# Zero padding of two short contraction parts (64 and 48 rows) to 128 rows in a two-layer decoder kernel

## The reference

```python
# layer 1 attention (latent): T = 128 tokens, 16 heads, HEAD_DIM = 128 + 64
q = rmsnorm(hidden @ q_a_w, q_a_ln_w) @ q_b_w        # 256 -> 192 -> 16 * 192
kv_raw = hidden @ kv_a_w                             # 64 latent + 16 * 64 rope
kv_latent = rmsnorm(kv_raw[..., :64], kv_a_ln_w)
kv = (kv_latent @ kv_b_w).reshape(B, T, 16, 128 + 128)
scores = einsum('bqhd,bkhd->bhqk', q, concat(k_nope, k_rope)) * scale
...
return attn @ o_w

# layer 1 feed forward (mixture), I = 176, 8 experts, top 2
shared_out = sigmoid(x @ shared_gate.T) * (x @ shared_up.T) @ shared_down.T   # contraction over 176
return x + shared_out + routed
x = _layernorm(x + ...)
```

## Time and profile before

| | |
|---|---|
| median of 3 runs | 1812.41 us |
| the three runs | 1812.41, 1830.32, 1805.54 us |
| profiled execution | 1830.32 us, span 1830.1 us |
| PE busy | 1487.3 us (81%), 9568 matmuls |
| DVE, ACT, POOL busy | 944.2, 585.0, 498.8 us |
| mean granted TensorE clock | 0.868 of full speed |

### The profile page before, as it was taken

The page is one execution under the profiler, slowest core; times in us unless marked ns, Lnnn a source line. Parts: engine busy times, 40 slices in busy tenths (PEclk is TensorE's granted clock), DMA queues, the critical chain, the costliest instruction groups (busy, mean ns, idle before and its releaser), DMA issues. The chain is left out here.

```text
span 1830.1 us, 33017 instructions
## 1 busy us (share of the span) xinstructions
PE 1487.3 (81%) x9568; PEld 1027.2 (56%) x9568; DVE 944.2 (52%) x2501; ACT 585.0 (32%) x1370; POOL 498.8 (27%) x1027
## 2 busy tenths in 40 slices
PE   1563899699996444439999999999999699997897
PEld 1562566355553222217788778888787355553565
DVE  6874465355553899952334324232234355553776
ACT  1464344144442222212222212222122144443453
POOL 6343477321211222221212211131112122221232
PEclk7677899799999676667999979797889699998999
DMA  8289565322221001020001000010000222221111
GB/s 239 80 255 232 161 200 176 99 78 77 86 77 41 26 26 32 26 64 4 18 21 32 17 17 22 18 29 17 17 14 27 69 84 78 85 79 59 35 47 42
DMA packets 148702, 128.43 MB, mean 70 GB/s; under 512 B 13360, under 2 KB 127344, under 8 KB 148640
## 3 DMA queue, kind: packets, MB, share of 16 engines
q1 hardware_dynamic: 142880, 116.46, 21.6%
q0 software_dynamic: 4320, 10.88, 2.3%
q10 hardware_dynamic: 1440, 0.33, 0.1%
HBM read 83.59 MB, written 46.20 MB: 71 GB/s over the span
## 5 line engine op out<-in xcount | busy, mean ns | idle before, releaser
L412 DVE TENSOR_REDUCE ca_nm<-ca_p_s 128x2 f32<-128x512 f32 x256 | 176.1, 690 | 223.4 <-PE ca_p_s L320 219.9
L355 PE MATMUL ca_p_o<-ca_pt,ca_va 128*32 128x256 f32 x1024 | 254.1, 386 | 0.7 <-ACT ca_pt L545 0.7
L545 ACT ACTIVATE ca_pt<-ca_p_e 128x512 f32<-128x512 f32 x256 | 152.1, 597 | 162.3 <-PE ca_p_e L342 160.9
L1945 PE MATMUL la_p_f<-la_qt,q_w 128*128 128x128 f32 x512 | 142.8, 366 | 13.2 <-ACT la_lt L2094 11.9
L355 PEld LDWEIGHTS ca_p_o<-ca_pt,ca_va 128*32 128x32 f32 x1024 | 90.9, 109 | 103.8 <-issue 46.3
L1946 PE MATMUL la_p_f<-la_qt,q_w 64*128 64x128 f32 x512 | 144.5, 368 | 0.0
L340 PE MATMUL ca_p_e<-ca_qs,ca_ks 96*128 96x256 bf16 x512 | 128.5, 277 | 0.1
L342 PE MATMUL ca_p_e<-ca_mt,row_of 96*128 96x256 bf16 x512 | 126.8, 274 | 0.0
L320 PE MATMUL ca_p_s<-ca_ks,ca_qs 96*128 96x256 bf16 x512 | 101.8, 283 | 28.2 <-DMA ca_ks<-k_stack 26.3
L2113 ACT ACTIVATE la_pq<-la_p_s,la_nm 128x128 f32<-128x128 f32 x256 | 73.0, 368 | 153.9 <-DVE la_nm L2153 153.9
L1945 PEld LDWEIGHTS la_p_f<-la_qt,q_w 128*128 128x128 f32 x512 | 88.7, 217 | 50.0 <-ACT la_lt L2094 16.9
(11 more groups left out here) (301 smaller groups left out, 3275.9 us busy)
## 6 DMA issues: line engine op xcount, KB each, us to landing
ca_qs<-q_stack SPq DMA_DIRECT2D x64, 192.0 KB, 2.6
ca_ks<-k_stack SPq DMA_DIRECT2D x64, 192.0 KB, 2.9
k_stack<-qkv_stack SPq DMA_DIRECT2D x16, 384.0 KB, 3.1
qa_stack<-qkv_stack SPq DMA_DIRECT2D x16, 384.0 KB, 3.3
ka_stack<-qkv_stack SPq DMA_DIRECT2D x16, 384.0 KB, 3.3
sa_qs<-qa_stack SPq DMA_DIRECT2D x32, 192.0 KB, 2.6
sa_ks<-ka_stack SPq DMA_DIRECT2D x32, 192.0 KB, 3.0
ca_ct<-in_ctx_t SPq DMA_DIRECT2D x32, 128.0 KB, 3.1
```

The source lines that it names most:

```text
L355: last = pe.matmul(p_o[rows, h // 4, :], VA[u][:, kc, h, :], PT[h % 2][:, kc, :], start=(kc == 0), stop=(kc == 1))
L412: dve.tensor_reduce(NM[u][:, h, :], p_s[h % 2][:, :, :], AX.X, ALU.max, negate=True).then_inc(max_done, 1)
L545: act.activation(PT[h % 2][:, :, :], p_e[h % 2][:, :, :], ACT.Exp, scale=SCALE).then_inc(exp_done, 1)
L1945: pe.matmul(bank[:, 128 * j:128 * j + 128], sh.q_w[:, 0, h, :], QT[:, 0, :], start=True, stop=False)
```

## The change

The 64-row part of the query products and the 48-row part of the shared down product get 128 rows, with zeros in the rows that are new. `sh.q_w` gets its upper half of part 1 set to zero once, in preparation, by POOL; `QN` is widened to 256 columns whose last 64 are set to zero once, so that its second transpose gives 128 rows; ACT copies both parts to `QT` with one instruction. In the mixture `SD`'s second part is set to zero ahead of its load, which therefore moves behind a wait on POOL and behind the load of `XR[0]`; `HS` is widened in the same way, and ACT copies `HST` with one instruction. The waits on the constants are raised to match.

```diff
@@ set_constants
+        pool.memset(sh.q_w[64:128, 1, :, :], 0.0).then_inc(const_set, 1)
+        pool.wait_ge(const_set, CONSTANTS)
-CONSTANTS = 16
+CONSTANTS = 17
@@ latent_attention
-        QN = sb("qn", [S, Q_LORA], F32)
+        QN = sb("qn", [S, 2 * 128], F32)
@@ pe: f4
+                if is_first(b):
+                    pe.wait_ge(const_ready, 3)
-                pe.transpose(p_f[0][0:64, 128:256], QN[:, 128:Q_LORA], sh.ident[:, :])
+                pe.transpose(p_f[0][:, 128:256], QN[:, 128:256], sh.ident[:, :])
@@ pe: queries
-                    last = pe.matmul(bank[:, 128 * j:128 * j + 128], sh.q_w[0:64, 1, h, :], QT[0:64, 1, :],
+                    last = pe.matmul(bank[:, 128 * j:128 * j + 128], sh.q_w[:, 1, h, :], QT[:, 1, :],
                                      start=False, stop=True)
@@ act: f4
-                act.activation(QT[:, 0, :], p_f[0][:, 0:128], ACT.Copy)
-                act.activation(QT[0:64, 1, :], p_f[0][0:64, 128:256], ACT.Copy)
+                act.activation(QT[:, :, :], p_f[0][:, 0:256].rearrange("p (c s) -> p c s", c=2), ACT.Copy)
@@ dve: norm_qa
-                dve.tensor_scalar(QN[:, :], ...)
+                dve.tensor_scalar(QN[:, 0:Q_LORA], ...)
@@ pool
+            pool.memset(QN[:, Q_LORA:256], 0.0).then_inc(const_ready, 1)
-            pool.wait_ge(const_ready, 2)
+            pool.wait_ge(const_ready, 3)
@@ mixture_feed_forward
-        HS = sb("hs", [S, EI], F32)
+        HS = sb("hs", [S, 2 * 128], F32)
@@ sp
+            sp.dma_start(XR[0][:, :], x_in[0]).then_inc(xr_loaded[0], 16)
+            sp.wait_ge(const_steps, 4)
             sp.dma_start(SD[0:EI - 128, 1, :], shared_down_t[128:EI]).then_inc(weights_loaded, 16)
-            sp.dma_start(XR[0][:, :], x_in[0]).then_inc(xr_loaded[0], 16)
@@ pe: turn_inner, down
-                    pe.transpose(p_k[0:EI - 128, 128:256], HS[:, 128:EI], sh.ident[:, :])
+                    pe.transpose(p_k[:, 128:256], HS[:, 128:256], sh.ident[:, :])
-                pe.matmul(p_x[:, 1, :], HST[0:EI - 128, 1, :], SD[0:EI - 128, 1, :], start=False,
+                pe.matmul(p_x[:, 1, :], HST[:, 1, :], SD[:, 1, :], start=False,
@@ act: copy_inner
-                    act.activation(HST[:, 0, :], p_k[:, 0:128], ACT.Copy)
-                    act.activation(HST[0:EI - 128, 1, :], p_k[0:EI - 128, 128:256], ACT.Copy).then_inc(inner_copied, 1)
+                    act.activation(HST[:, :, :], p_k[:, 0:256].rearrange("p (c s) -> p c s", c=2),
+                                   ACT.Copy).then_inc(inner_copied, 1)
@@ dve: inner_shared
-                dve.tensor_tensor(HS[:, :], p_s[:, EI:2 * EI], SSIG[:, :], ALU.mult).then_inc(shared_inner, 1)
+                dve.tensor_tensor(HS[:, 0:EI], p_s[:, EI:2 * EI], SSIG[:, :], ALU.mult).then_inc(shared_inner, 1)
@@ dve, pool
-            dve.wait_ge(const_steps, 2)
+            dve.wait_ge(const_steps, 4)
+            pool.memset(SD[:, 1, :], 0.0).then_inc(const_steps, 1)
+            pool.memset(HS[:, EI:256], 0.0).then_inc(const_steps, 1)
-            pool.wait_ge(const_steps, 2)
+            pool.wait_ge(const_steps, 4)
```

More of the change, by code:

```diff
@@ L2160, in norm_qa @@
                 wait(dve, pv_done, G * (b - 1))
-                dve.tensor_scalar(QN[:, :], p_f[1][:, 0:Q_LORA], RQ[:, 0:1], SCALE, ALU.mult, ALU.mult).then_inc(qa_normed, 1)
+                dve.tensor_scalar(QN[:, 0:Q_LORA], p_f[1][:, 0:Q_LORA], RQ[:, 0:1], SCALE, ALU.mult, ALU.mult).then_inc(qa_normed, 1)
                 dve.scalar_tensor_tensor(LL[u][:, 0:2 * LATENT].rearrange("p (n l) -> p n l", n=2),
```

## The result

The changed kernel takes 1685.35 us in the median of three runs (1680.31 to 1685.76), against 1812.41 before: ratio 0.9278, 95% interval 0.9223 to 0.9334. The profiled execution took 1680.31 us, with a span of 1678.5: 151.6 us less than the 1830.1 of before, where 144.7 us were forecast.

A forecast was written before the change was run, and what follows sets the result against it. PE was taken to set the latent stage's pace. Query stage 140.5, copy 1.0 and mixture 5.8, less 2.1 for the memset and 0.5 for the load, made 144.7 us: 1830.3 to 1685.6 us, range 1660 to 1716.

The forecast's parts named there:

- 0.19 us for each change between 64 and 128 rows: Latent query matmuls: each step between 64 and 128 rows costs 0.19 us beyond the pace of equal rows.
- Query matmuls at 0.115 us: Latent query stage: 64 padded matmuls at the rope's pace take 7.36 us, not 13.29; 5.93 us gained a batch.
- The falls of the clock: Latent query stages: no falls at the rope's density; four batches gain 15.28 us each, the first 14.2.
- The price of a fall: Latent batches: one holding a fall of the clock takes 43.92 us in place of 34.58, so 9.35 us.
- the falls stay: Rival, chance 0.08: the drains go but the clock still falls in some query stages; 1714 us.
- The reading that spread and falls are one: Runs before differ by falls in query stages, so the changed median is 1685 us; otherwise near 1668.
- No new wait: Latent batch of about 28.6 us: no new wait priced; as a rival, chance 0.04, about 1701 us.
- The columns: Transpose ahead of the queries: 64 stationary columns cost no more than 128, so widening costs and gains nothing.
- The mixture: Shared down product: 0.30 us and a merged copy's 0.06 gained a batch, 5.8 us; later load at start costs 0.5.
- Preparation: POOL's memset of q_w and a wait behind it put 2.1 us on the path, bounds 0 to 4.
- that nothing changes: Rival, chance 0.03: rows are free in query matmuls, padding saves nothing; 1812 us at the median.
- that full arrays lower the clock: Rival, chance 0.02: 128 active rows in all query matmuls hold the lower clock through the latent stage; 2060 us.

The follow-up runs named there:

- e1: The kernel before with only the changed kernel's part up to the latent stage, the mixture left old: 1685.91 us, ratio 0.934.
- e3: The kernel before, unpadded, reordered so that in each four heads the 128-row products go first, then the 64-row ones: 1706.76 us, ratio 0.946.
- e5: The kernel before with the first query product of each head also on 64 rows, the rest of its contraction left out: 1734.76 us, ratio 0.952.
- e9: The changed kernel with each head's second query product cut to 32 columns and not added to the first: 1759.29 us, ratio 0.966.
- e2: The kernel before with only the mixture's part of the change, the latent stage left old: 1819.72 us, ratio 1.010.
- e7: The changed kernel with each head's 32 weighing columns in both cross attentions put into 128, zero elsewhere: 1643.68 us, ratio 0.907.
- e6b: The changed kernel with POOL's memset of q_w moved behind the issues of the weight loads: 1681.96 us.

## Why the prediction was right

- **The step on which all rests, 0.19 us for each change between 64 and 128 rows, held.** It was read from starts in PE's timeline; `e1` shows that the latent part alone gives all but 4 to 5 us of the gain, and `e3` that the price goes with the changes and not with the 64-row matmul. Query matmuls at 0.115 us: measured 0.112, as a stage without the change is 6.09 us shorter and not 5.93. Eleven batches: 67.0 us against 65.2.
- **The falls of the clock went, as said**: four batches went from 43.92 to 28.21 us, 62.8 us against 61.1, and the first stage gave 14.4 against 14.2. The price of a fall was read a little low: 43.92 was set against 34.58, but the batches that hold the falls are of the kind that takes 34.35, so a fall cost 9.57 us and not 9.35.
- **The slow stretches outside the query stages were not in the sum.** The prediction said that the clock never falls in the stage's rope, score or projection matmuls. In the last batch it does: PE waits up to 0.89 us ahead of its weighings and then runs about ten us at clock 0.50, the projection among them. Another slow stretch lies behind the first query stage (1.5 us gained). These are the windows of the last batch from its last query matmul on, before and after:

```profile
1401.96:1433.10 31.14, 24.28 (x133) 20.54 (x132) 12.29 (x29) 5.64 (x18) 4.67 (x9) 0.82 0.06 18
```

```profile
1257.64:1285.20 27.56, 20.04 (x134) 17.27 (x131) 12.31 (x29) 5.64 (x18) 4.70 (x10) 0.98 0.07 20
```

  Both carry the same work; 3.6 us went with the clock. With some 0.5 us of copies and 0.6 lost at the stage's start the latent stage gained 149.1 us where 141.5 were forecast.
- **The agreement of the medians to 0.3 us is luck.** On the two profiled executions, for which the sum was made, it fell 6.9 us short: 7.6 too little for the latent stage, 1.5 too much for the mixture, 0.5 for preparation, and 1.3 us in stages that the change does not touch. The profiled execution of the changed kernel happened to be its fastest, 5 us below the median.
- **The reason for the clock was half right.** The prediction put it down to PE's density, and rival "the falls stay" to the wait or the weighing. `e5` and `e9` show that the rows in use matter by themselves. The forecast came out because padding mends both at once, and that is luck too. Had the change removed the standstills by using 64 rows throughout, the same reasoning would have missed some 50 us (`e5`: 1734.76 us).
- **The reading that spread and falls are one was borne out**, by `e2` and by the clocks of the runs of before: it is why 1685 was given and not 1668.
- **No new wait came.** PE's wait ahead of the queries fell from 0.82 to 0.78 us; 0.06 was put down, 0.04 measured. The widened transpose cost nothing.
- **The columns.** The prediction said that the trace agrees with the Trainium skill's rule of draining ("TensorEngine Tiling (Array Packing)", Key Properties) for rows and not for columns, by the single case of 64 columns in a transpose. That was too wide. That case stays free, but `e9` shows 12.04 - 7.22 = 4.82 us for 32 changes between 128 and 32 columns, 0.15 us each, and `e7` a gain where they go. For those the trace agrees with the rule.
- **The mixture was sized too high, and its start too low**: 5.8 - 0.5 = 5.3 us forecast, 3.8 measured in its stage. PE's timeline, to be set beside the earlier trace rows:

```profile
1592.29 0.60 PE L2508 MATMUL mf_p_x<-mf_sd,mf_hst 128*128 128x256 f32 x2
1592.72 0.60 PE L2509 MATMUL mf_p_x<-mf_sd,mf_hst 128*128 128x256 f32 x2
1593.15 0.61 PE L2489 MATMUL mf_p_h<-identb,mf_he 128*128 128x128 bf16 x8
...
1596.25 1.47 PE L2465 MATMUL mf_p_s<-mf_ws,mf_xt 128*128 128x360 f32 x4 [0.52 <-ACT mf_xt L2541]
```

  The pair of pairs takes 0.86 us as said, 0.30 less. The batch went from 7.97 to 7.66 us (L2508 to L2508, the next at 1599.95), 0.31 and not 0.36, 5.0 us over sixteen: ACT's merged copy did not add to it. At the start of the stage PE waits for the same load as in the earlier trace rows:

```profile
1545.07 2.74 PE L2465 MATMUL mf_p_s<-mf_ws,mf_xt 128*128 128x360 f32 x4 [3.02 <-DMA mf_sd<-in_shared_down_t]
```

  From the stage's first load that is 5.87 us where it was 4.80, 1.07 us later and not 0.5: the load of `SD`'s second part was issued 0.48 us later, as said, and took 3.5 us to land where it took 2.8. Together 3.9 us, about what the stage shows. The starts spread too: three profiles with the old order of loads have 4.80 to 5.37 us here, four with the new one 5.60 to 5.87.
- **Preparation**: +2.6 us to the first load of self attention, against 2.1 put down. The delay of POOL by 1.90 us is shown; that it is what moved the stage is not (`e6b`), as versions with the same preparation differ by up to 4 us.

The rivals: that the falls stay is out, as none of sixteen stages holds one; that nothing changes is out by the result, and `e3` says why; that full arrays lower the clock is turned round by `e5`, in which it fell with 64 rows at the pace at which it held with 128.

## What to carry to other kernels

Look for neighbours on PE whose row counts lie on both sides of the half array, or whose columns go between 32 and 128: a start-to-start time that is longer than that of equal neighbours is the sign. The length of a weight load does not show it (189 ns in the median for 128 rows beside 184 for 64), and that of a matmul shows it only in part (302 and 322 ns where equal rows have 275). Zeros in the short operand cost PE nothing here, and 96 rows did as well as 128; where padding is not possible, sort like with like. If the clock falls in a stage in which PE looks busy, see how many rows its matmuls use and how far apart they start; and if runs of one kernel spread by some per cent, compare their mean clocks and look for such stages in the traces before calling it noise.

## What the runs showed of the hardware that was not expected

- The clock fell from its upper to its lower level in six of sixteen stages in which PE ran 64-row matmuls without a gap (0.112 us each), and in none of sixteen in which it ran 128-row matmuls, every second pair on 32 columns, with gaps (0.19 us each).
- Matmuls on 96 and on 128 rows follow each other at 0.112 us; between 64 and 128 rows each change costs 0.18 to 0.19 us, between 32 and 128 columns 0.15 us.
- Two neighbours on different groups of 32 columns cost the time of one: eight in 0.99 us where four took 0.98.
